# A fused attention and feed-forward kernel: a new order on all five queues, the branch turned, xn's high half on VectorE, dummy products at the start, a tail by tile

## The chip, the cores and the metric

The kernel runs on one core of one Trainium2 chip. The metric is the device time of one execution in microseconds. The core's engines are TensorE (PE, with its weight loads PEld), VectorE (DVE), ScalarE (ACT), GpSimd (POOL) and SyncE (SP), which here issues all DMAs. Each has its own queue and works it off in order; they meet through semaphores.

## What is computed

For sixteen sequences of 512 rows with 128 features, float32:

```python
x = x + layernorm(attention(layernorm(x)))       # scores = (xn*w_lhs) @ (xn*w_rhs)^T, softmax, @ xn
h = silu(t(x2, w1) * s1) * (t(x2, w2) * s2)      # x2 = layernorm(x), 128 -> 512
h = gelu(t(h, h1) * sh1)                         # 512 -> 512
h = gelu(t(h, h2) * sh2)                         # 512 -> 512
x = x + layernorm(t(h, w3) * s3)                 # 512 -> 128
```

`t` multiplies by a matrix whose entries are -1, 0 or 1. There is no gain or bias in the layer norms.

## The kernel before

Every sequence b is one unit of work of N = 16; it is held as T = 4 tiles of 128 rows, and the hidden 512 features as K = 4 blocks of 128. To keep float32 accuracy each operand of a product is split into a high half that the array takes exactly and a low remainder: ScalarE makes the high half by a copy (`high_xT`, `high_aT`, `high_e`, `high_A`, `high_x2T`, the first of the two instructions of each `gelu`), VectorE or GpSimd the low one by a subtraction (`low_xT`, `low_aT`, `low_e`, `low_A`, `low_B`, `low_x2T` on VectorE, `low_C` and `low_xn` on GpSimd), and TensorE adds the products (`product`, L341).

The path of one sequence: SP loads x (`load_x`); VectorE takes statistics (`x_statistics`, `aggregate`), GpSimd the reciprocal root (`rstd`, L1995), VectorE normalises by tile (`normalize_x`, L1579), TensorE turns the tiles (`turn_x`), and `scores` (L309) makes four 128x512 blocks of scores, three products each. VectorE takes each block's row maximum (`row_max`), ScalarE the exponential (`softmax`), TensorE turns the result (`turn_e`), and `attend` (L325) multiplies it with xn, split into two fp16 halves: `xn_hi` (GpSimd's `high_xn`, L2014) and `xn_lo`. Both exist once, so `high_xn(b)` waits (`wait_free` on `pv_done`) until all `attend` of sequence b - 1 are done. Then come a layer norm (`attention_statistics`, `rstd_att`, `normalize_att`), the sum x1 (`add_attention`), another norm (`normalize_x1`), `turn_x2`, and the feed-forward part: `gated` (L356, four products into a pair of banks; `silu` on ScalarE, `gated` on VectorE), `layer1` and `layer2` (sixteen pairs of products each, `gelu1`, `gelu2` between), `layer3`, `scale_y`, `turn_y`, the last norm and `add_ffn` on GpSimd, and `store`. ScalarE loads a table at each change between exponential, silu and gelu.

The work of neighbouring sequences is interleaved in an order written out by hand for every engine: `start()`, then a loop `Fori(5, N - 3)` over `step(i)`, whose calls belong to the sequences i to i - 4 (`now`, `back1`, ...; `ahead` on VectorE), then `finish()`. Nothing reorders a queue at run time. On TensorE `start()` stands before a branch: the sum of the weights' low bits (`sum_lo` on ScalarE for each of six parts of the weights, `gather_lo`, `total_lo`) is loaded into a register; it is zero for these weights; if it weren't, `main(general=True)` would run, with a third product per pair. `main` holds `ramp()`, the loop and `finish()`, and both bodies are in the program one behind the other:

```python
pe.wait_ge(lo_known, 1)
any_lo = pe.value_load(lo_total[0:1, 0:1].bitcast(i32))
with pe.If(any_lo != 0):
    main(general=True)
with pe.Else():
    main(general=False)
```

SP's `start()` issues x(0), x(1), x_res(0), the columns and then the six parts of the weights (512 KB each but the last, which has 256 KB; an x has 256 KB, the columns 9.5 KB). ScalarE's `start()` begins with `sum_lo(0)`, `high_xT(0)`, `high_aT(0)`. At the end the last sequence goes through `layer3` with `low_C` on GpSimd, `turn_y`, `y_statistics`, `rstd`, `normalize_y`, `add_ffn` of the whole [128, 4, 128] tile, and one store.

## Time and profile before

| what | value |
|---|---|
| median of 3 runs | 511.75 us (511.27 to 512.38) |
| the profiled execution | 512.09 us |
| its span, first to last instruction | 510.3 us |
| PE busy | 479.0 us, 94%, 2818 products |
| ACT busy | 447.9 us, 88% |
| DVE busy | 384.9 us, 75% |
| POOL busy | 245.7 us, 48% |
| mean granted clock of TensorE | 0.986 |

The span and what lies around it (1.8 us) make the execution's time. Busy products overlap each other on TensorE, so its pace is read from their starts. Times in the rows count from the span's start.

### The profile page before, as it was taken

How to read it: one execution, taken by the hardware profiler on the slowest of the kernel's cores; microseconds unless marked ns; L12 is line 12 of the kernel's file. 1: busy time of each engine (PE TensorE's matmuls, PEld its weight loads, DVE VectorE, ACT ScalarE, POOL GpSimd, SP SyncE). 2: the span in 40 equal slices, each digit the busy share in tenths (PEclk: the TensorE clock that was granted, in tenths of full speed). 3: DMA queues.
4: the chain of work that ended last, by engine and by line, in shares of the span. 5: the costliest groups of instructions: out<-in, count | busy, mean ns of one | idle time of the engine just before them, and what ended most of it. 6: DMA issues, size and time to landing. Idle time of an engine off the chain costs nothing.

```text
span 510.3 us, 9417 instructions
## 1 busy us (share of the span) xinstructions
PE 479.0 (94%) x2818; PEld 385.3 (76%) x2818; DVE 384.9 (75%) x1154; ACT 447.9 (88%) x749; POOL 245.7 (48%) x270
## 2 busy tenths in 40 slices
PE   2959999999999999999999999999999999999992
PEld 1747888888888888888888888878787788787771
DVE  4968979697786969698686969878688777475552
ACT  4968999998999999898999999898989999786771
POOL 3635773634445473535455453445624316143444
PEclk9979999999999999999999999999999999999997
DMA  8020101202011100202121110111101100010111
GB/s 299 12 85 1 63 1 42 83 2 102 21 62 41 62 21 22 81 21 62 41 62 38 42 44 21 63 41 43 62 4 59 42 3 21 1 62 2 62 43 62
DMA packets 12557, 24.23 MB, mean 47 GB/s; under 512 B 1520, under 2 KB 1520, under 8 KB 12528
## 3 DMA queue, kind: packets, MB, share of 16 engines
q1 hardware_dynamic: 12528, 23.87, 14.0%
q8 instruction: 15, 0.25, 0.2%
q14 instruction: 14, 0.11, 0.1%
HBM read 15.48 MB, written 8.39 MB: 47 GB/s over the span
## 4 chain that ended last, share of the span: by engine, by line
PE 81%; ACT 9%; issue 4%; DVE 3%; DMA 1%; POOL 1%; SPq 0%; POOLq 0%; ACTq 0%; DVEq 0%
PE hid_bank L345 21%; PE hid_bank L347 21%; PE score_bank L294 5%; PE mix_bank L331 3%; PE hid_bank L366 3%; PE mix_bank L332 3%; PE mix_bank L335 3%; PE score_bank L313 3%; PE hid_bank L371 2%; PE hid_bank L370 2%; PE hid_bank L367 2%; PE score_bank L319 2%; PE score_bank L316 2%; PE w_bank L303 2%; PE w_bank L347 2%
## 5 line engine op out<-in xcount | busy, mean ns | idle before, releaser
L345 PE MATMUL hid_bank<-hA_hi,w_hi 128*128 128x512 f32 x256 | 105.9, 414 | 1.2 <-DVE hA_full L1503 1.2
L345 PE MATMUL hid_bank<-hB_hi,w_hi 128*128 128x512 f32 x256 | 105.3, 412 | 1.6 <-DVE hB_lo L1577 1.6
L347 PE MATMUL hid_bank<-hB_lo,w_hi 128*128 128x512 f32 x256 | 101.1, 395 | 0.0
L347 PE MATMUL hid_bank<-hA_lo,w_hi 128*128 128x512 f32 x256 | 100.7, 393 | 0.0
L2026 POOL TENSOR_TENSOR hC_lo<-hC_full,hC_hi 128x512 fp32r<-128x512 f32 x64 | 81.2, 1294 | 22.9 <-ACT hC_full L1163 22.8
L1499 DVE TENSOR_REDUCE neg_max<-score_bank 128x1 f32<-128x512 f32 x56 | 38.3, 687 | 41.6 <-PE score_bank L319 40.6
L1503 DVE SCALAR_TENSOR_TENSOR hA_full<-hid_bank,columns,gate 128x512 f32<-128x512 f32 x64 | 46.7, 746 | 19.1 <-ACT gate L1156 18.3
L345 PEld LDWEIGHTS hid_bank<-hB_hi,w_hi 128*128 128x128 f32 x256 | 48.2, 188 | 11.7 <-DVE hB_lo L1577 2.7
L345 PEld LDWEIGHTS hid_bank<-hA_hi,w_hi 128*128 128x128 f32 x256 | 48.2, 188 | 11.5 <-DVE hA_full L1503 2.5
L347 PEld LDWEIGHTS hid_bank<-hB_lo,w_hi 128*128 128x128 f32 x256 | 48.4, 189 | 9.7 <-DVE hB_lo L1577 0.9
L1998 POOL TENSOR_SCALAR ln_y_var_eps<-ln_y_mean_var 128x4 f32<-128x4 f32 x16 | 5.8, 360 | 102.1 <-DVE ln_y_mean_var L1494 102.1
L347 PEld LDWEIGHTS hid_bank<-hA_lo,w_hi 128*128 128x128 f32 x256 | 48.3, 189 | 8.6
L1577 DVE TENSOR_TENSOR hB_lo<-hid_bank,hB_hi 128x512 fp32r<-128x512 f32 x64 | 43.4, 680 | 13.4 <-ACT hid_bank L1163 13.1
L1162 ACT ACT_TABLE_LOAD x29 | 37.2, 1283 | 16.1 <-PE hid_bank L347 15.7
L1162 ACT ACTIVATE hC_hi<-hid_bank,columns 128x512 fp32r<-128x512 f32 x64 | 44.6, 697 | 7.4 <-PE hid_bank L347 6.0
L1162 ACT ACTIVATE hB_hi<-hid_bank,columns 128x512 fp32r<-128x512 f32 x64 | 44.8, 701 | 3.7 <-PE hid_bank L347 3.4
L1573 DVE TENSOR_TENSOR hA_lo<-hA_full,hA_hi 128x512 fp32r<-128x512 f32 x64 | 44.1, 693 | 1.1 <-ACT hA_hi L1143 0.9
L1163 ACT ACTIVATE hC_full<-hid_bank,columns 128x512 f32<-128x512 f32 x64 | 44.4, 693 | 0.0
L1156 ACT ACTIVATE gate<-hid_bank,columns 128x512 f32<-128x512 f32 x64 | 42.4, 685 | 2.2 <-PE hid_bank L371 1.8
L1163 ACT ACTIVATE hid_bank<-hid_bank,columns 128x512 f32<-128x512 f32 x64 | 43.1, 673 | 0.0
L1131 ACT ACT_TABLE_LOAD x28 | 35.9, 1283 | 6.4 <-DVE neg_max L1499 5.3
L1569 DVE TENSOR_TENSOR eT_lo<-score_bank,eT_hi 128x512 f16<-128x512 f32 x56 | 38.2, 682 | 3.5 <-ACT eT_hi L1137 3.5
(105 smaller groups left out, 1216.8 us busy)
## 6 DMA issues: line engine op xcount, KB each, us to landing
x_res<-x_dram SPq DMA_DIRECT2D x16, 256.0 KB, 2.8
out_dram<-x SPq DMA_DIRECT2D x16, 256.0 KB, 2.0
x_tail<-out_dram SPq DMA_DIRECT2D x16, 256.0 KB, 3.0
out_dram<-y_out SPq DMA_DIRECT2D x16, 256.0 KB, 2.0
x_in<-x_dram SPq DMA_DIRECT2D x15, 256.0 KB, 2.6
w_raw<-weights_dram SPq DMA_DIRECT2D x5, 512.0 KB, 5.9
x_ahead<-x_dram SPq DMA_DIRECT2D x1, 256.0 KB, 2.9
w_raw<-weights_dram SPq DMA_DIRECT2D x1, 256.0 KB, 5.7
```

The source lines that it names most:

```text
L345: nc.tensor.matmul(bank[:, :], w_hi[:, w], hi, start=first, stop=False)
L347: mm = nc.tensor.matmul(bank[:, :], w_hi[:, w], lo, start=False, stop=last and not general)
L1131: nc.scalar.activation(exps[:, j, :], score_home(b, j)[:, :], ACT.Exp, bias=neg_max[:, j:j + 1], scale=-1.0, accum_out=row_sum[:, j:j + 1] ...
L1156: nc.scalar.activation(gate[:, m % 2, :], hid_bank[2 * (m % 2)][:, :], ACT.Silu, scale=columns[:, S1 + m:S1 + m + 1]).then_inc(gate_ready, 1)
L1162: nc.scalar.activation(hi[:, m, :], hid_bank[m][:, :], ACT.Gelu, scale=scale)
L1163: nc.scalar.activation(full, hid_bank[m][:, :], ACT.Gelu, scale=scale).then_inc(done, 1)
L1499: nc.vector.tensor_reduce(neg_max[:, j:j + 1], score_home(b, j)[:, :], AX.X, ALU.min).then_inc(max_ready, 1)
L1503: nc.vector.scalar_tensor_tensor(hA_full[:, m, :], hid_bank[2 * (m % 2) + 1][:, :], columns[:, S2 + m:S2 + m + 1], gate[:, m % 2, :], ALU. ...
L1569: nc.vector.tensor_tensor(eT_lo[:, j, :, :].rearrange("p t s -> p (t s)"), score_home(b, j)[:, :], eT_hi[:, j, :, :].rearrange("p t s -> p ...
L1573: nc.vector.tensor_tensor(hA_lo[:, m, :], hA_full[:, m, :], hA_hi[:, m, :].bitcast(f32), ALU.subtract).then_inc(hA_lo_ready, 1)
L1577: nc.vector.tensor_tensor(hB_lo[:, m, :], hid_bank[m][:, :], hB_hi[:, m, :].bitcast(f32), ALU.subtract).then_inc(hB_lo_ready, 1)
L2026: nc.gpsimd.tensor_tensor(hC_lo[:, m, :], hC_full[:, m, :], hC_hi[:, m, :].bitcast(f32), ALU.subtract).then_inc(hC_lo_ready, 1)
```

## The change

All queues get a new order. Beside the order these parts are new: the branch is turned; `warm_up` puts dummy products before and behind the first turn; `high_xn` moves from GpSimd to VectorE; the last sequence's `low_C` moves to VectorE, and its last norm, sum and store go tile by tile. Six pieces move ahead of the branch: `scores(2, 0)`, `scores(2, 1)`, `attend(1, 2)`, `attend(1, 3)`, `turn_e(2, 0)` and `turn_x2(0)`. The loop of every engine is cut at another place: an iteration of TensorE's begins with `layer1(back4, 0, 0)` and ends with `turn_y(back4)`.

```diff
@@ SP
+            def store_tiles(g):
+                for t in range(T):
+                    sp.wait_ge(y_tile_ready, t + 1)
+                    sp.dma_start(x_view(out_dram, g)[:, t, :], y_out[:, t, :]).then_inc(out_stored, 16)
             def start():
                 load_x(0)
-                load_x(1)
-                load_x_res(0)
                 load_columns()
                 load_weights(0)
+                load_x(1)
                 load_weights(1)
                 load_weights(2)
+                load_x(2)
                 load_weights(3)
-                load_x(2)
+                load_x_res(0)
                 load_weights(4)
                 load_weights(5)
...
-                store(N - 1)
+                store_tiles(N - 1)
@@ TensorE
+            def warm_up(count):
+                for _ in range(count):
+                    nc.tensor.matmul(score_bank[0][:, 0:P], ident[:, :], ident[:, :], start=True, stop=True)
             def start():
+                warm_up(11)
                 turn_x(0)
+                warm_up(5)
                 scores(0, 0)
...
                 attend(1, 0)
+                turn_e(1, 2)
+                scores(2, 0)
+                turn_e(1, 3)
+                attend(1, 1)
                 gather_lo()
-                attend(1, 1)
-                turn_e(1, 3)
+                scores(2, 1)
+                attend(1, 2)
+                attend(1, 3)
+                turn_e(2, 0)
+                pe.wait_ge(xT_lo_ready, 6)
+                turn_x2(0)
@@ TensorE, step(i): the head and the end of the new loop
+                    pe.wait_ge(gated_done, back4 * K + 3)
+                    layer1(general, back4, 0, 0)
+                    pe.wait_ge(gated_done, back4 * K + 3)
+                    layer1(general, back4, 1, 0)
                     layer1(general, back4, 0, 1)
+                    pe.wait_ge(yT_ready, back1 - 3)
+                    turn_x(back1)
...
                     gated(general, back3, 3)
+                    pe.wait_ge(e_lo_ready, back1 * T + 2)
+                    scores(back1, 3)
                     pe.wait_ge(att_n_ready, back4 + 3)
                     turn_y(back4)
@@ TensorE, the branch
-            with pe.If(any_lo != 0):
+            with pe.If(any_lo == 0):
+                main(general=False)
+            with pe.Else():
                 main(general=True)
-            with pe.Else():
-                main(general=False)
@@ VectorE
+            def high_xn(b):
+                dve.wait_ge(xn_ready, b + 1)
+                wait_free(dve, pv_done, T, b, 0)
+                nc.vector.tensor_copy(xn_hi[:, :, :], xn[:, :, :]).then_inc(xn_hi_ready, 1)
+            def low_C(b, m):
+                dve.wait_ge(hC_lo_ready, b * K)
+                dve.wait_ge(gelu2_done, b * K + m + 1)
+                nc.vector.tensor_tensor(hC_lo[:, m, :], hC_full[:, m, :], hC_hi[:, m, :].bitcast(f32), ALU.subtract).then_inc(hC_lo_ready, 1)
+            def normalize_and_add_y(b):
+                dve.wait_ge(ln_y.rstd_ready, b + 1)
+                dve.wait_ge(y_ready, b)
+                dve.wait_ge(x1_tail_loaded, b * 16 + 16)
+                dve.wait_ge(out_stored, b * 16)
+                for t in range(T + 1):
+                    if t < T:
+                        nc.vector.tensor_scalar(y_n[:, t, :], y_bank[:, t * P:(t + 1) * P], ln_y.mean_var[:, t, 0:1],
+                                                ln_y.rstd[:, t:t + 1], ALU.subtract, ALU.mult).then_inc(y_tile_normalized, 1)
+                    if t > 0:
+                        dve.wait_ge(y_tile_normalized, t)
+                        nc.vector.tensor_tensor(y_out[:, t - 1, :], y_n[:, t - 1, :], x1_tail[:, t - 1, :],
+                                                ALU.add).then_inc(y_tile_ready, 1)
@@ VectorE, step(i): what follows aggregate(ln_x, ahead) in the new loop
+                low_e(back1, 2)
+                low_xT(now)
+                low_e(back1, 3)
                 low_aT(now)
                 low_B(back3, 1)
+                low_B(back3, 2)
+                high_xn(now)
+                row_max(now, 0)
+                low_B(back3, 3)
+                row_max(now, 1)
+                attention_statistics(back1)
                 normalize_x1(back2, 0)
                 normalize_x1(back2, 1)
+                normalize_x(ahead, 0)
@@ VectorE, finish()
+                low_C(N - 1, 0)
+                low_C(N - 1, 1)
+                low_C(N - 1, 2)
+                low_C(N - 1, 3)
                 y_statistics(N - 1)
                 aggregate(ln_y, N - 1)
-                normalize_y(N - 1)
+                normalize_and_add_y(N - 1)
@@ GpSimd
-            def high_xn(b):
-                pool.wait_ge(xn_ready, b + 1)
-                wait_free(pool, pv_done, T, b, 0)
-                apart(pool)
-                nc.gpsimd.tensor_copy(xn_hi[:, :, :], xn[:, :, :]).then_inc(xn_hi_ready, 1)
@@ ScalarE, start(): the head
                 sum_lo(0)
                 high_xT(0)
                 high_aT(0)
                 sum_lo(2)
-                high_weights(2)
-                sum_lo(1)
+                high_weights(0)
                 softmax(0, 0)
-                high_weights(5)
                 softmax(0, 1)
                 softmax(0, 2)
```

In the finish two places of the order matter to the prediction. Between `gated(N - 6, 0)` and `gated(N - 6, 2)` stand now `scores(N - 4, 2)` and `scores(N - 4, 3)` (before: neither), between `gated(N - 5, 0)` and `gated(N - 5, 2)` stands `scores(N - 3, 2)` (before: `turn_e(N - 3, 1)`), and between `gated(N - 4, 0)` and `gated(N - 4, 2)` no scores and no `turn_e` (before: `scores(N - 2, 2)` and `turn_e(N - 2, 1)`). ScalarE's `softmax(N - 1, 0)` and `softmax(N - 1, 1)` stand between `silu(N - 3, 1)` and `silu(N - 3, 2)` (before: between two gelus).

## Rows read from the trace of the kernel before

**Rows 1.** Windows: stretch, length, busy us per engine (instructions), PEclk, DMA share, GB/s.
```profile
0.00:15.00 15.00, 6.06 (x15) 4.04 (x16) 7.79 (x30) 8.38 (x15) 5.21 (x15) 1.00 0.74 263
30.00:40.00 10.00, 4.85 (x36) 4.10 (x35) 5.97 (x20) 5.57 (x9) 3.56 (x4) 0.66 0.34 105
80.00:320.00 240.00, 240.00 (x1454) 196.50 (x1453) 194.19 (x595) 226.81 (x379) 118.69 (x131) 1.00 0.14 45
320.00:460.00 140.00, 137.40 (x810) 109.99 (x807) 105.61 (x297) 126.23 (x210) 60.46 (x67) 1.00 0.11 37
460.00:502.00 42.00, 38.57 (x167) 29.04 (x165) 19.92 (x57) 30.43 (x48) 19.82 (x19) 1.00 0.09 32
```

**Rows 2.** Timeline of TensorE, the turn of y in two iterations six apart.
```profile
135.09 0.60 PE L294 MATMUL mix_bank<-ident,yT 128*128 128x128 f32 x4
310.18 0.60 PE L294 MATMUL mix_bank<-ident,yT 128*128 128x128 f32 x4
```

**Rows 3.** Timeline of the first 13 us: start, us, engine, line, tiles.
```profile
1.21 0.29 POOL L2050 TENSOR_SCALAR_AFFINE_SELECT ident<-ident 128x128 f32<-128x128 f32 x1
4.96 0.87 DVE L1484 BATCH_NORM_STATS2 ln_x_stats<-x_ahead 128x6 f32<-128x128 f32 x4
6.40 1.12 DVE L1584 TENSOR_SCALAR xn<-x_in,ln_x_mean_var,ln_x_rstd 128x128 f32<-128x128 f32 x4 [0.57 <-POOL ln_x_rstd L2011]
6.89 1.15 PE L303 MATMUL w_bank<-ident,xn 128*128 128x128 f32 x4 [6.89 <-DVE xn L1584]
7.83 1.06 ACT L1190 ACTIVATE hA_full<-w_raw 128x1024 f32<-128x1024 uint16 x1 [5.61 <-DMA w_raw<-weights_dram]
10.08 0.69 DVE L1479 TENSOR_TENSOR xT_lo<-w_bank,xT_hi 128x512 fp32r<-128x512 f32 x1 [1.76 <-ACT aT_hi L1124]
12.07 0.63 PE L313 MATMUL hid_bank<-xT_hi,aT_hi 128*128 128x512 f32 x1
12.50 0.63 PE L316 MATMUL hid_bank<-xT_lo,aT_hi 128*128 128x512 f32 x1
```

**Rows 4.** Timeline of VectorE and TensorE around the branch, 32 to 41 us.
```profile
32.21 1.11 DVE L1592 TENSOR_SCALAR x2n<-x,ln_x_mean_var,ln_x_rstd 128x128 f32<-128x128 f32 x4
35.40 0.79 PE L313 MATMUL score_bank<-xT_hi,aT_hi 128*128 128x512 f32 x1 [5.15 <-issue]
37.09 0.69 DVE L1499 TENSOR_REDUCE neg_max<-score_bank 128x1 f32<-128x512 f32 x1 [3.77 <-PE score_bank L319]
38.56 0.69 DVE L1479 TENSOR_TENSOR x2T_lo<-w_bank,x2T_hi 128x512 fp32r<-128x512 f32 x1 [0.18 <-ACT x2T_hi L1183]
39.97 0.39 PE L367 MATMUL hid_bank<-x2T_hi,w_hi 128*128 128x512 f32 x1
40.20 0.40 PE L370 MATMUL hid_bank<-x2T_lo,w_hi 128*128 128x512 f32 x1
```

**Rows 5.** Groups by form, whole run: busy us, mean ns, idle before.
```profile
L1592 DVE TENSOR_SCALAR x2n<-x,ln_x_mean_var,ln_x_rstd 128x128 f32<-128x128 f32 x64 | 19.0, 341 | 0.1
L2026 POOL TENSOR_TENSOR hC_lo<-hC_full,hC_hi 128x512 fp32r<-128x512 f32 x64 | 81.2, 1294 | 22.9 <-ACT hC_full L1163 22.8
L2018 POOL CAST xn_hi<-xn 128x512 f16<-128x512 f32 x16 | 9.8, 613 | 35.2 <-PE mix_bank L335 18.7 <-issue 15.2 <-DVE xn L1584 1.3
L1162 ACT ACT_TABLE_LOAD x29 | 37.2, 1283 | 16.1 <-PE hid_bank L347 15.7
```

**Rows 6.** TensorE's waits from 320 to 502 us: total, times, longest.
```profile
PE hid_bank L366 <- DVE hA_full L1503: 2.3, 3, 1.0
```

**Rows 7.** Timeline of the last 12 us, four engines.
```profile
498.13 0.68 ACT L1163 ACTIVATE hC_full<-hid_bank,columns 128x512 f32<-128x512 f32 x1
500.20 0.49 PE L347 MATMUL w_bank<-hC_lo,w_hi 128*128 128x512 f32 x1 [0.84 <-POOL hC_lo L2026]
505.17 1.36 DVE L1523 TENSOR_SCALAR y_n<-mix_bank,ln_y_mean_var,ln_y_rstd 128x128 f32<-128x128 f32 x4 [1.52 <-POOL ln_y_rstd L2011]
507.90 0.34 SPq L213 DMA_DIRECT2D out_dram<-y_out  x1
```

More of the change, by code:

```diff
@@ L525, in ramp @@
                     gated(general, 1, 0)
+                    pe.wait_ge(gelu2_done, 4)
+                    gated(general, 1, 1)
                     pe.wait_ge(x2T_lo_ready, 2)
@@ L1715, in start @@
-                low_A(1, 2)
-                low_A(1, 3)
-                aggregate(ln_y, 0)
-                x_statistics(5)
-                low_xT(4)
-                normalize_y(0)
-                normalize_x1(2, 1)
-                low_e(3, 2)
-                low_B(1, 0)
-                aggregate(ln_x, 5)
-                low_aT(4)
-                low_B(1, 1)
-                low_e(3, 3)
-                normalize_x1(2, 2)
-                row_max(4, 0)
-                scaled_eps(3)
-                normalize_x1(2, 3)
@@ L1732, in start @@
-                row_max(4, 1)
+                low_A(1, 2)
+                aggregate(ln_y, 0)
+                low_A(1, 3)
+                x1_statistics(2)
+                x_statistics(5)
+                normalize_y(0)
+                aggregate(ln_x1, 2)
+                low_B(1, 0)
+                low_e(3, 2)
+                low_xT(4)
+                low_e(3, 3)
+                low_aT(4)
+                scaled_eps(3)
+                low_B(1, 1)
+                aggregate(ln_x, 5)
+                high_xn(4)
@@ L1847, in finish @@
                 gated(N - 5, 3)
-                row_max(N - 3, 2)
                 low_A(N - 5, 2)
                 row_max(N - 3, 3)
-                normalize_x1(N - 4, 1)
-                y_statistics(N - 6)
-                low_A(N - 5, 3)
-                aggregate(ln_y, N - 6)
-                x_statistics(N - 1)
-                low_xT(N - 2)
-                scaled_eps(N - 3)
-                aggregate(ln_x, N - 1)
-                normalize_y(N - 6)
-                low_B(N - 5, 0)
-                low_e(N - 3, 2)
@@ L1862, in finish @@
-                low_aT(N - 2)
-                low_B(N - 5, 1)
-                low_e(N - 3, 3)
+                y_statistics(N - 6)
+                aggregate(ln_y, N - 6)
+                low_A(N - 5, 3)
+                x1_statistics(N - 4)
+                low_xT(N - 2)
+                aggregate(ln_x1, N - 4)
+                low_e(N - 3, 2)
+                normalize_y(N - 6)
+                x_statistics(N - 1)
+                scaled_eps(N - 3)
+                normalize_x1(N - 4, 0)
+                normalize_x1(N - 4, 1)
@@ L1865, in finish @@
+                low_B(N - 5, 0)
+                low_aT(N - 2)
+                normalize_x1(N - 4, 2)
+                normalize_x1(N - 4, 3)
+                low_e(N - 3, 3)
+                low_B(N - 5, 1)
+                aggregate(ln_x, N - 1)
+                row_max(N - 2, 0)
+                row_max(N - 2, 1)
                 low_B(N - 5, 2)
-                row_max(N - 2, 0)
                 low_B(N - 5, 3)
-                row_max(N - 2, 1)
                 attention_statistics(N - 3)
-                normalize_x1(N - 4, 2)
@@ L1883, in finish @@
+                high_xn(N - 2)
+                low_A(N - 4, 0)
+                gated(N - 4, 2)
+                gated(N - 4, 3)
+                low_A(N - 4, 1)
+                row_max(N - 2, 2)
+                normalize_x(N - 1, 0)
+                low_A(N - 4, 2)
+                low_A(N - 4, 3)
+                y_statistics(N - 5)
+                x1_statistics(N - 3)
+                low_B(N - 4, 0)
                 low_e(N - 2, 1)
+                normalize_x(N - 1, 1)
+                low_B(N - 4, 1)
@@ L2091, in step @@
                 back2 = i - 2
+                back3 = i - 3
                 back4 = i - 4
-                rstd(ln_x, now)
-                high_xn(back1)
-                low_xn(back1)
-                rstd_att(back2)
-                low_C(back4, 0)
-                low_C(back4, 1)
-                low_C(back4, 2)
                 low_C(back4, 3)
```

1121 lines of the change are left out of this document (540 added, 581 removed).

## The prediction, made before the changed kernel was run

> **What bounds the kernel now.** I read the windows of the whole run first [rows 1]. From 80 to 320 us TensorE is busy 240.0 of 240.0 us, while ScalarE has 226.8 us of work in them, VectorE 194.2 and GpSimd 118.7. So the middle is TensorE's throughput, and only its own work or a wait of its own can change it. One sequence takes there (310.18 - 135.09) / 6 = 29.18 us [rows 2], and sixteen of them are 467 us. The span is 510.3 us, so some 43 us lie elsewhere, and the windows say where: TensorE is idle 9 of the first 15 us, 5 of the ten from 30 to 40 us, some 3 of 320 to 460, over 3 of 460 to 502, and nearly all of the last 8 to 9 us. The change can earn something in the ramp, in the finish and in the tail, and lose something in all four parts.
>
> The ramp in order of time. The first product of a score waits for the first block of weights: ScalarE's queue begins with a sum over w_raw, which starts when that lands, at 7.83, and holds back ScalarE's two copies of the turned x; VectorE's xT_lo waits for the second, aT_hi, until 10.08 [rows 3]. Products there start 0.43 us apart (12.07 to 12.50), 0.23 later on (39.97 to 40.20), the slower of the clock's two levels against the faster [rows 3, 4]. From then on VectorE is hardly idle until its last x2n tile ends at 32.21 + 1.11 = 33.3. At 30.2 TensorE reaches the branch on the weights' low bits, and its next product starts at 35.40 after 5.15 us in which it waited for nothing that the profile shows; VectorE then idles 3.77 us for that product's result, and the granted clock over 30 to 40 us is 0.66 [rows 1, 4]. The first feed-forward group's second product starts at 39.97.
>
> **The change part by part.** My sum is against the profiled execution, 512.09 us (span 510.3 and 1.8 around it), 0.34 above the median of the three runs, 511.75.
>
> Branch. With the condition turned, the general=False body follows the branch directly and the branch moves behind turn_x2(0). What remains of the 5.15 us there is unknown: at most all of it, at least the register load alone. I take the lower end, under 1 us, and it is covered: after turn_x2(0) TensorE must wait for ScalarE's copy and VectorE's difference (some 0.6 and 0.7 us) anyway. The Trainium skill, "Runtime: NRT & Kernel Launch", section "Instruction fetch mechanics", says that a taken branch out of the fetched pages stalls for a fetch and that sequential code is fetched ahead; by that rule only the old order pays. At the end of the program TensorE now must jump over the other body; it has 8.4 us for that while the tail runs (501.9, some 1.7 us behind the product on hC_lo, to 510.3), against 5.15 us, so this costs nothing, and with no tail it would cost the 5.
>
> But the 5.15 us are not all gained, for VectorE is late next. VectorE's low_x2T(0) ends before at 38.56 + 0.69 = 39.25, and the third product of gated(0,0), which needs it, starts at 40.20 [rows 4]. In the new order VectorE finishes the first four tiles at 7.5, then does the negated weights (0.3, an estimate like one tile's instruction), statistics (0.9), high_xn(0) (0.5) and an aggregate (0.4, a third of four such tiles' 1.11): low_xT(0) at 9.6 instead of 10.1 [rows 3, 4], if the first weights land before the turn is done. They should: 256 KB + 9.5 KB stand before them instead of three times 256 KB and 9.5 KB. From low_xT(0) to its last x2n tile the old order needs 33.3 - 10.1 = 23.2 us [rows 3, 4]. The new one needs these and, before low_x2T(0): high_xn(1) and (2) at 0.5 each, row_max(2,0), row_max(2,1) and low_e(1,3) at 0.6, one more set of statistics 0.9, and low_x2T 0.7, which is 27.6. It ends at 37.2, and the third product can start there instead of at 40.20: 3.0 us. By then TensorE has also done scores(2,1) and turn_e(2,0), three products at 0.23 and four turns at some 0.1, which before stood behind: 1.1 us more work done. Ramp: 3.0 + 1.1 = 4.1 us. The ends are 1.5 (GpSimd's or ScalarE's queue is late in it) and 6 (VectorE's new order has fewer holes than the old one's 23.2 us).
>
> Dummy products. Eleven before the first turn and five behind it, on the identity, into a score bank that nobody uses yet. They lie between 1.5 us (identity ready) and 6.89, when the first tile is there, and then in the hole of over 2 us before aT_hi. Nearest rows: a turn at the slower level, 1.15/4 = 0.29, and a full product there, 0.43 [rows 3]; at 0.43 eleven take 4.7 us and are done at 6.3. So they cost nothing; if each takes 0.86 (two full passes), eleven end at 11 and push the first turn by 4 us. Their gain is the faster level from about 7 us, 0.2 us on each of the 9 products until 15, nearly all of it hidden behind VectorE's row maxima.
>
> The moved rounding. GpSimd's cast of 0.61 us becomes a VectorE copy. Bounds: one normalised 128x128 tile, 0.34, and a 512-wide difference, 0.69 [rows 3, 5]. I take 0.5. Sixteen are 8 us on an engine that is idle 46 us of the 240. The Trainium skill, "VectorE: DVE Perf Modes", section "The perf-mode tier table (the rule you actually need)", lets an fp32 copy in SBUF run at twice the rate of a two-input operation; by it the copy would be near the lower end and the ramp 0.3 us shorter. GpSimd loses 0.61 us of 29.18 that nobody waited for. The new wait matters more: high_xn(now) waits in VectorE's queue for all attend of the sequence before, and behind it stand low_B(back3,3) and the row maxima. Writing the new loop beside TensorE's order at 0.23 a product, attend ends about 12 us into the iteration, VectorE comes to the copy at about 12.5, and low_B(.,3) is wanted at 16. Nothing is lost, with 2 us of cover. The tighter hand-overs of the loop, low_A(.,3) before layer1(.,0,3), low_aT before scores and low_e(.,3) before attend(.,3), have 0.5 us each. Counted in the code, the loop keeps nine groups of short products among the long ones, as before, and five table loads. So I leave 29.18 us.
>
> Finish. The largest of TensorE's waits there are three, 2.3 us in all, at gated(.,2) for VectorE's gate [rows 6]. In the first two sequences of the new finish a scores group (0.7 us) stands between gated(.,0) and gated(.,2) that stood before them, or behind; in the third the filler is 1.1 us thinner. ScalarE gets one more table load of 1.28 us (73 in the old order, 74 in the new, counted in the code) [rows 5]. I take a gain of 0.5, with ends -2 and +2.5.
>
> Tail. low_C(N-1,.) moves from GpSimd (1.29) to VectorE (0.69): the last hC_full ends at 498.81, the product on hC_lo starts at 500.20 [rows 5, 7], and would at 498.9 + 0.7 = 499.6: 0.6. Normalising begins at 505.17 and takes 1.36 us, and behind it the whole-tile sum on GpSimd some 1.3, for the store is issued at 507.90; interleaved on VectorE, four tiles at 0.34 and four sums at 0.2 (my estimate: a third of the 0.69 for a quarter of its columns) end at 507.35: 0.5. The store takes from 507.90 to the end; a last piece of 64 KB instead of 256 KB gives between 0 and 0.5, I take 0.3. Sum 1.4. SP issues each piece in 0.34 us [rows 7] while VectorE needs 0.5 a tile, so its queue isn't late.
>
> Sum: 4.1 + 0.5 + 1.4 = 6.0; 512.1 - 6.0 = 506.1.
>
> **The rivals.** (1) VectorE binds in the loop. For: in its order the long stretch from gated(.,2) to the row maxima has no hole for 16 us and hand-overs of 0.5. Against: it is idle 19% from 80 to 320 us. If 0.3 us a sequence leaks in eight loops and three of the finish, 3.3 us go: 509.4. (2) Slower: at high_xn's wait. Its place is VectorE's queue between low_B(.,2) and low_B(.,3). It decides if attend ends over 2 us later against VectorE than I count, or if the stretch behind it runs 0.5 us late and ScalarE, with 94.5% of the time in work, can't make it good. At 0.7 us a sequence in eleven it costs 7.7: 513.8. (3) The branch costs as before, because it is the register load or the branch itself and not where it leads. Then 5 us stand before gated(0,0) with 1.3 of cover, and the slower clock again 1.5; the ramp loses 1 instead of gaining 4: 511. The Trainium skill's "SBUF — State Buffer", on the shared port pair, lets a two-port VectorE copy block GpSimd for its length; by it each early copy could hold a reciprocal root by up to 0.5 us, and the ramp would gain 3.1. (4) Better: ramp 6, finish 2, tail 1.6: 502.5.
>
> **How the numbers follow.** Forecast 506.1 with 0.55; (1) 0.15; (2) 0.08; (3) 0.06; (4) 0.16. The range leaves out (2), half of (3) and the best end of (4): 502.4 to 510.5. Under 0.2%, 1.0 us, a measurement here can't tell from no change. Faster is all of the forecast, (1) and (4), less a little: 0.85; same mostly (3): 0.07; slower 0.08.
>
> **What would show it.** Right: a gap of under 1.5 us around the branch and products 0.23 apart behind it; gated(0,0) near 37; turn_y to turn_y still 29.18; xn_hi on VectorE near 0.5; the last store issued near 502. Wrong: TensorE waits between 80 and 320 us (rival 1 or 2, told apart by whether VectorE idles before xn_hi); 5 us at the branch (3); the first turn later than 6.9 (dummies too long).

## The result, and the profile of the kernel after

| what | before | after |
|---|---|---|
| median | 511.61 us (511.27 to 512.38, 4 runs) | 508.32 us (508.14 to 508.9, 4 runs) |
| the profiled execution | 512.09 us | 508.16 us |
| its span | 510.3 us | 506.4 us |
| mean granted clock | 0.986 | 0.991 |
| first product of gated(0,0) | 39.64 us | 34.88 us |
| period of the loop | 29.18 us | 29.47 us |

The change is faster by 0.7%: ratio 0.993, 95% interval 0.9916 to 0.9944. The forecast was 506.1 (502.4 to 510.5); the profiled execution stands 2.1 us above it. 3.9 us of span were gained and not 6.0.

The windows that answer to [rows 1], and that from 15 to 30 us, kernel after (stretch, length, busy us per engine, PEclk, DMA share, GB/s):

```profile
0.00:15.00 15.00, 12.32 (x68) 10.06 (x68) 9.23 (x33) 9.22 (x18) 4.44 (x13) 1.00 0.74 263
15.00:30.00 15.00, 12.39 (x97) 9.83 (x96) 14.51 (x46) 13.68 (x29) 8.42 (x8) 0.89 0.12 29
30.00:40.00 10.00, 9.18 (x83) 7.45 (x82) 9.75 (x40) 9.31 (x18) 5.96 (x6) 1.00 0.18 66
80.00:320.00 240.00, 240.00 (x1463) 194.16 (x1462) 194.65 (x594) 222.10 (x374) 114.17 (x124) 1.00 0.14 44
```

From 30 to 40 us TensorE is busy 9.2 us instead of 4.9. From 80 to 320 us it is "busy" all 240.0 in both kernels, and yet an iteration got longer: busy products overlap, so a wait of 0.1 to 0.2 us between two of them doesn't show in this column. Only the starts show it. The turn of y in two iterations seven apart, timeline of TensorE, kernel after:

```profile
100.99 0.60 PE L299 MATMUL mix_bank<-ident,yT 128*128 128x128 f32 x4
...
307.29 0.60 PE L299 MATMUL mix_bank<-ident,yT 128*128 128x128 f32 x4
```

(307.29 - 100.99) / 7 = 29.47 us, against 29.18 in [rows 2]: 0.29 us lost in each of eight iterations.

The ramp, timeline of the kernel after, the first 13 us (compare [rows 3]):

```profile
1.57 4.54 PE L410 MATMUL score_bank<-ident 128*128 128x128 f32 x22 [1.57 <-POOL ident L2091]
...
6.03 1.06 ACT L1201 ACTIVATE hA_full<-w_raw 128x1024 f32<-128x1024 uint16 x1 [3.80 <-DMA w_raw<-weights_dram]
...
8.15 0.41 DVE L1594 CAST xn_hi<-xn 128x512 f16<-128x512 f32 x1
...
9.01 0.69 DVE L1489 TENSOR_TENSOR xT_lo<-w_bank,xT_hi 128x512 fp32r<-128x512 f32 x1 [0.16 <-ACT aT_hi L1135]
...
10.75 0.40 PE L318 MATMUL hid_bank<-xT_hi,aT_hi 128*128 128x512 f32 x1
...
10.99 0.39 PE L321 MATMUL hid_bank<-xT_lo,aT_hi 128*128 128x512 f32 x1
```

Eleven dummies are 22 instructions and end at 6.1 us, the copy of xn takes 0.41, xT_lo starts at 9.0 instead of 10.1, and the first scores' products start 0.23 to 0.24 apart (0.43 in [rows 3]). Around the branch, timeline of VectorE and TensorE, kernel after (compare [rows 4]):

```profile
32.47 1.11 DVE L1621 TENSOR_SCALAR x2n<-x,ln_x_mean_var,ln_x_rstd 128x128 f32<-128x128 f32 x4
...
33.46 0.60 PE L308 MATMUL w_bank<-ident,x2n 128*128 128x128 f32 x4
...
34.77 0.69 DVE L1489 TENSOR_TENSOR x2T_lo<-w_bank,x2T_hi 128x512 fp32r<-128x512 f32 x1
34.88 0.47 PE L371 MATMUL hid_bank<-x2T_hi,w_hi 128*128 128x512 f32 x1 [0.82 <-ACT x2T_hi L1194]
...
35.51 0.50 PE L375 MATMUL hid_bank<-x2T_lo,w_hi 128*128 128x512 f32 x1
```

The branch lies between 33.46 and 34.88, and what TensorE waits for there is ScalarE's x2T_hi. In the trace's records of control instructions the register load takes 0.49 us (at 33.62) and the compare-and-branch 0.09 (at 34.17); before they took 0.57 and 4.67. The branch back to the loop's head, which is taken too but leads less far, takes 0.21 to 0.25 us in both kernels. At the end of the program the jump over the other body takes 3.28 us, from 498.19, while the tail runs. The third product of gated(0,0) starts at 35.51 and not at 40.20.

The tail, timeline of the kernel after (compare [rows 7]):

```profile
496.80 0.50 PE L352 MATMUL w_bank<-hC_lo,w_hi 128*128 128x512 f32 x1 [0.30 <-DVE hC_lo L1628]
...
501.79 0.73 DVE L1566 TENSOR_SCALAR y_n<-mix_bank,ln_y_mean_var,ln_y_rstd 128x128 f32<-128x128 f32 x2 [1.53 <-POOL ln_y_rstd L2058]
...
502.74 2.02 SPq L219 DMA_DIRECT2D out_dram<-y_out  x4
...
503.47 0.49 DVE L1570 TENSOR_TENSOR y_out<-y_n,x_tail 128x128 f32<-128x128 f32 x2
```

**Where the time went.** Spans against spans: turn_y(1) comes at 100.99 instead of 105.89, and by then the new order has also done the three products of a scores block (0.70 us) that stood behind it: 5.6 us ahead, with one loop iteration in it, so the ramp gained 5.9. The eight iterations lost 8 x 0.29 = 2.3. From turn_y(8) to the last product it is 191.7 us before and 191.2 after; with the 0.70 of the scores block off, that is 0.2 lost, although low_C on VectorE gave 0.5 there: the finish itself lost 0.7. Behind the last product 8.39 us became 7.85: 0.5. Sum 5.9 - 2.3 - 0.7 + 0.5 + 0.5 = 3.9.

### The profile page after: what moved, and what is told of

Same layout as the page of the kernel before. It is cut to its first block, busy times and chain, and to the rows that moved or that the text cites. A ratio compares the mean times of both kernels' runs of the same rounds, so it can differ in the third digit from the quotient of the medians.

```text
span 506.4 us, 9435 instructions
## 1 busy us (share of the span) xinstructions
PE 486.3 (96%) x2850; PEld 387.8 (77%) x2850; DVE 394.4 (78%) x1178; ACT 447.9 (88%) x750; POOL 228.8 (45%) x249
## 3 DMA queue, kind: packets, MB, share of 16 engines
HBM read 15.48 MB, written 8.39 MB: 47 GB/s over the span
## 4 chain that ended last, share of the span: by engine, by line
PE 70%; ACT 13%; DVE 11%; issue 4%; DMA 1%; POOL 0%; POOLq 0%; DVEq 0%; ACTq 0%
PE hid_bank L350 19%; PE hid_bank L352 18%; PE score_bank L299 4%; ACT hC_full L1174 3%; PE hid_bank L371 3%; PE score_bank L318 3%; PE mix_bank L340 2%; PE hid_bank L375 2%; PE mix_bank L336 2%; PE hid_bank L376 2%; PE hid_bank L372 2%; PE w_bank L308 2%; PE mix_bank L337 2%; PE w_bank L352 2%; PE score_bank L321 2%
## 5 line engine op out<-in xcount | busy, mean ns | idle before, releaser
L350 PE MATMUL hid_bank<-hB_hi,w_hi 128*128 128x512 f32 x256 | 104.0, 406 | 1.3 <-DVE hB_lo L1606 1.2
L2067 POOL TENSOR_TENSOR hC_lo<-hC_full,hC_hi 128x512 fp32r<-128x512 f32 x60 | 76.4, 1293 | 30.0 <-ACT hC_full L1174 29.9
L352 PEld LDWEIGHTS hid_bank<-hB_lo,w_hi 128*128 128x128 f32 x256 | 48.3, 189 | 10.7 <-DVE hB_lo L1606 1.2
L1173 ACT ACT_TABLE_LOAD x29 | 37.2, 1283 | 16.6 <-PE hid_bank L352 16.4
L1602 DVE TENSOR_TENSOR hA_lo<-hA_full,hA_hi 128x512 fp32r<-128x512 f32 x64 | 45.4, 715 | 0.7 <-ACT hA_hi L1154 0.5
L1174 ACT ACTIVATE hid_bank<-hid_bank,columns 128x512 f32<-128x512 f32 x64 | 44.2, 691 | 0.0
```

The costliest lines, as they stand in the source:

```text
L350: nc.tensor.matmul(bank[:, :], w_hi[:, w], hi, start=first, stop=False)
L352: mm = nc.tensor.matmul(bank[:, :], w_hi[:, w], lo, start=False, stop=last and not general)
L1173: nc.scalar.activation(hi[:, m, :], hid_bank[m][:, :], ACT.Gelu, scale=scale)
L1174: nc.scalar.activation(full, hid_bank[m][:, :], ACT.Gelu, scale=scale).then_inc(done, 1)
L1602: nc.vector.tensor_tensor(hA_lo[:, m, :], hA_full[:, m, :], hA_hi[:, m, :].bitcast(f32), ALU.subtract).then_inc(hA_lo_ready, 1)
L2067: nc.gpsimd.tensor_tensor(hC_lo[:, m, :], hC_full[:, m, :], hC_hi[:, m, :].bitcast(f32), ALU.subtract).then_inc(hC_lo_ready, 1)
```

## The experiments

Twelve kernels ran. Each leaves out nothing of the computation. Ratios are against the kernel before on the same chip. "Period" is the loop's period, read as above from the turns of y; "g0" is the start of gated(0,0).

**e1: ScalarE's high_e(back1, 0) earlier.** In the loop of the kernel after, VectorE waits 26.9 us in 8 iterations for eT_hi.

```diff
                 gelu2(back4, 0)
-                gelu2(back4, 1)
                 high_e(back1, 0)
+                gelu2(back4, 1)
                 high_x2T(back3)
```

> The changed kernel with one line of ScalarE's loop moved: high_e(back1, 0) ahead of gelu2(back4, 1) instead of behind it. Theory A (the loop's 29.47 us instead of 29.18 come from that hand-over: VectorE stands 3.4 us before low_e(back1, 0) and scores(back1, 2) starts late): the iteration goes back to 29.2 us, eight iterations give 2.2 us, so 506.0 to 506.3. Theory B (VectorE has too much work since it has the copy to fp16, rival 1 of the prediction): the iteration stays at 29.4 to 29.5 and the time at 508.3. Theory C (nine groups of short products stand in places with dearer weight loads): also 29.4 or more.

Measured: 507.87 us (507.17 to 508.55), ratio 0.9924 (0.9907 to 0.9941); period 29.464. The first wait went, the time did not. Another took its place in every iteration, at the second pair of the feed-forward gate. Timeline of e1, VectorE and TensorE:

```profile
155.97 1.41 DVE L1513 SCALAR_TENSOR_TENSOR hA_full<-hid_bank,columns,gate 128x512 f32<-128x512 f32 x2 [1.45 <-ACT gate L1167]
...
156.32 0.40 PE L352 MATMUL w_bank<-hC_lo,w_hi 128*128 128x512 f32 x1
156.77 0.50 PE L371 MATMUL hid_bank<-x2T_hi,w_hi 128*128 128x512 f32 x1
157.11 0.40 PE L372 MATMUL hid_bank<-x2T_hi,w_hi 128*128 128x512 f32 x1
```

The two products at 156.32 and 156.77 start 0.45 apart, 0.22 more than a pair without a wait: gated(back3, 2) needs the bank that VectorE's multiplication at 155.97 reads. Also the next start is 0.34 behind it and not 0.23.

**e2: the branch not turned, all else as after.**

```diff
-            with pe.If(any_lo == 0):
-                main(general=False)
-            with pe.Else():
-                main(general=True)
+            with pe.If(any_lo != 0):
+                main(general=True)
+            with pe.Else():
+                main(general=False)
```

> The changed kernel with the branch as before it (general=True first, the other body behind Else). If the 5.15 us belong to where the branch leads, a hole of some 5 us opens behind the register load at 34.2 us, of which 0.6 us are covered by the wait for x2T_hi, and the products behind it run at the slower level of the clock for some us: 512.5 to 514.5. If the stall was the register load or the place of the branch, nothing changes: 508.3.

Measured: 511.79 us (510.35 to 513.42), ratio 0.9998 (0.9983 to 1.0014), g0 37.18, turn_y(0) at 75.41 instead of 71.46. The branch takes 3.34 us, the register load 0.48. Without the turned branch the whole change gives nothing that can be measured.

**e3: no dummy products.**

```diff
-                warm_up(11)
                 turn_x(0)
-                warm_up(5)
                 scores(0, 0)
```

> The changed kernel without the sixteen dummy products. By my prediction's step (VectorE's row maxima hide the gain) 0.3 us or less is lost: 508.3 to 508.6. If the faster level in the first 13 us carries the ramp's surplus over my forecast (6.2 us instead of 4.1), 1.5 us or more is lost: 509.8 to 510.5.

Measured: 509.94 us (508.77 to 510.62), ratio 0.9957 (0.9941 to 0.9973), g0 37.57, turn_y(0) at 74.17. Timeline of TensorE in e3:

```profile
9.18 0.80 PE L318 MATMUL hid_bank<-xT_hi,aT_hi 128*128 128x512 f32 x1 [1.26 <-ACT aT_hi L1133]
...
12.01 0.63 PE L324 MATMUL hid_bank<-xT_hi,aT_lo 128*128 128x512 f32 x1
12.44 0.63 PE L318 MATMUL hid_bank<-xT_hi,aT_hi 128*128 128x512 f32 x1
...
14.57 0.63 PE L324 MATMUL hid_bank<-xT_hi,aT_lo 128*128 128x512 f32 x1
```

The start is the same (9.18 against 9.03), but the last of the first twelve score products starts at 14.57 instead of 12.6: at 3 x 0.43 = 1.3 us a block, where a row maximum takes 0.6. So in this ramp TensorE, not VectorE, is the slow one between 9 and 15 us. The ratio says 1.4 us and g0 2.7; the same ramp gave g0 between 34.3 and 35.8 in the profiles of e1, e8, e9 and e11, so this one is good for a size of 1.4 to 2.7.

**e4: xn_hi back on GpSimd.**

```diff
-            def high_xn(b):
-                dve.wait_ge(xn_ready, b + 1)
...
+            def high_xn(b):
+                pool.wait_ge(xn_ready, b + 1)
+                wait_free(pool, pv_done, T, b, 0)
+                apart(pool)
+                nc.gpsimd.tensor_copy(xn_hi[:, :, :], xn[:, :, :]).then_inc(xn_hi_ready, 1)
```

> The changed kernel with high_xn taken back to GpSimd, each directly ahead of its low_xn there. If VectorE's added work is what the loop lost (theory B), the iteration falls to 29.2 us: 506.3. If the hand-over of high_e is the cause (theory A), the iteration stays at 29.47 and the time at 508.3 or a little less, as VectorE's copy of 0.41 us is hidden; GpSimd's 0.61 us ahead of rstd_att and low_C can also cost up to 1 us in ramp or finish: 507.8 to 509.3.

Measured: 507.38 us (507.01 to 508.53), ratio 0.992 (0.9903 to 0.9938), period 29.467, g0 34.48. The copy on VectorE is not what lengthens the loop, and moving it earned nothing that can be measured. The g0 lies within the scatter of this ramp. By the Trainium skill, "SBUF — State Buffer", section "Who interferes with whom", a two-port copy of VectorE and a GpSimd instruction contend for a shared pair of ports: the one that is issued first has it for its whole length, and the other waits. No run here shows the copy holding up GpSimd. The other way round it is there once in the kernel after, timeline of GpSimd and VectorE:

```profile
51.04 4.72 POOL L2085 TENSOR_TENSOR w_lo<-w_raw,w_hi 128x1024 fp32r<-128x1024 f32 x2
...
55.15 0.89 DVE L1594 CAST xn_hi<-xn 128x512 f16<-128x512 f32 x1
```

This copy starts while GpSimd works and takes 0.89 us instead of 0.41 to 0.43; it ends 0.28 us behind GpSimd's operation (55.76), and so it does, by 0.28 to 0.29, in e1, e2, e3, e8, e9 and e11. That agrees with the rule.

**e5, e6, e7: one part each, put on the kernel before.** Branch turned alone; tail by tile with low_C on VectorE alone; dummies alone. e5 is e2's diff the other way round, e7 e3's. e6:

```diff
-                store(N - 1)
+                store_tiles(N - 1)
...
-                normalize_y(N - 1)
+                normalize_and_add_y(N - 1)
```

> The kernel before with the branch turned and nothing else. VectorE and ScalarE idle 3.8 and 4.2 us behind the branch there, but low_aT(2) ends only at 32.3, so scores(2, 0) can start at 31.1 and its third product at 32.3 instead of 36.4, and the clock stays at the faster level: a gain of 3 to 4.5 us, 507.2 to 508.7. If so, the branch alone gives about what the whole change gave. If the stall is the register load, 511.6.

> The kernel before with low_C(N-1, .) on VectorE and the last norm, sum and store by tile. My step was 1.4 us: 510.2. From the trace after, where the span from the last turn to the end is 7.9 instead of 8.4 us and the wait for hC_lo 0.3 instead of 0.8: 1.0 to 1.1, so 510.5.

> The kernel before with the sixteen dummy products. Its turned x waits for ScalarE's sum over the first weights anyway, and VectorE's maxima follow one another: 0 to 0.8 us gained, 510.8 to 511.6.

Measured: e5 508.64 us (508.17 to 509.29), ratio 0.9944 (0.9922 to 0.9966), g0 34.95, period 29.197. e6 510.73 (509.18 to 512.3), ratio 0.9981 (0.9966 to 0.9996), span 508.9, which is 1.4 us less (0.2 of it by turn_y(1), where e6 is the kernel before; 0.6 before and 0.7 behind the last product belong to the tail). e7 511.92 (511.02 to 512.92), ratio 0.9999 (0.9984 to 1.0014), g0 39.10. The branch alone brings gated(0,0) 4.7 us forward, of which 3.9 are left at the end of the span (0.5 of the rest go behind the last product, which no run takes apart); window of e5, 30 to 40 us, against 4.85 and 0.66 in [rows 1]:

```profile
30.00:40.00 10.00, 8.62 (x59) 6.54 (x58) 9.47 (x29) 9.70 (x16) 7.32 (x6) 1.00 0.31 105
```

In the old ramp the dummies are worth nothing that can be measured.

**e8, e9: the chain through the row maximum shortened.** In the loop of the kernel after ScalarE waits 10.7 us in 7 iterations for neg_max. e8 moves one block of scores, e9 has e1's edit too.

```diff
                     attend(back2, 2)
-                    attend(back2, 3)
                     pe.wait_ge(e_lo_ready, back1 * T - 1)
                     scores(back1, 0)
+                    attend(back2, 3)
```

> The kernel after, with scores(back1, 0) put one attend earlier in TensorE's loop (ahead of attend(back2, 3), where the old loop has it). Theory A, a ring: row_max(back1, 0) and with it softmax(back1, 0) come some 0.7 us earlier in every iteration, ScalarE's wait for neg_max (10.7 us in 7 iterations, 1.5 each) falls to about 0.8, high_e(back1, 0) ends 0.7 earlier, TensorE's late starts at scores(back1, 2) and gated(back3, 2) go, and the period from turn_y to turn_y falls from 29.47 to 29.2: 2 us less over the loop. Theory B, the new loop's period is set by the order of its products (exposed weight loads between short and long ones), not by a chain: the period stays within 0.05 of 29.47, whatever ScalarE waits.

> Both edits on the kernel after: scores(back1, 0) ahead of attend(back2, 3), and high_e(back1, 0) ahead of gelu2(back4, 1). By itself the second left the period at 29.46, since a wait of 0.2 us at gated(back3, 2) took the place of the one at scores(back1, 2). Theory A (ring): with the scores early too neither wait is left, and the period is 29.2 or less, the time some 505.9 against 508.3 of the kernel after. Theory B (order of products): 29.4 or more.

Measured: e8 509.23 us (508.76 to 510.14), ratio 0.9955 (0.994 to 0.9969), period 29.557; e9 509.65 (508.04 to 510.09), ratio 0.9955 (0.9941 to 0.9969), period 29.567. The loop got 0.09 us longer. Two things show. First, one more block of long products after short ones costs 0.09 us: the second of its products starts 0.31 us behind the first, not 0.23. Second, the scores came 0.7 us earlier, but the row maximum didn't. VectorE in e9, timeline:

```profile
143.16 0.43 DVE L1594 CAST xn_hi<-xn 128x512 f16<-128x512 f32 x1 [0.86 <-PE mix_bank L340]
143.50 0.68 DVE L1509 TENSOR_REDUCE neg_max<-score_bank 128x1 f32<-128x512 f32 x1
```

Here the moved rounding does hold VectorE up, for the end of attend(back2, 3), and the row maximum queues behind it. This is the prediction's rival at high_xn's wait, made real by 0.7 us of other order; in the kernel after VectorE waits only 0.1 us there (0.08 to 0.12).

**e11, e12: that hold-up taken away.** e11 is e9 with the row maximum ahead of the copy; e12 is e9 with the copy on GpSimd.

```diff
                 low_B(back3, 2)
-                high_xn(now)
                 row_max(now, 0)
+                high_xn(now)
                 low_B(back3, 3)
```

> As e9 (scores(back1, 0) ahead of attend(back2, 3), high_e(back1, 0) ahead of gelu2(back4, 1)), and on VectorE row_max(now, 0) ahead of high_xn(now). In e9 VectorE idles 0.86 us before xn_hi, for the end of all attend, and row_max(.,0) stands behind it, at 143.50 against 143.37 in the kernel after: the early scores earned nothing. Theory A (ring through scores, row maximum, softmax, with the moved copy as the hold-up in e9): row_max(.,0) starts some 1 us earlier, ScalarE's wait for neg_max falls from 13.1 us to under 7 in 7 iterations, the wait at gated(back3, 2) goes, and the period is 29.30 (floor of before 29.19 plus 0.09 for one more entry from short into long products). Theory B (only the order of the products counts): 29.56 as in e8 and e9. If the copy's late end now delays something instead (turn of the pair attend, low_xn), the period is above 29.56.

> As e9, with high_xn on GpSimd as in the kernel before, so that nothing waits for the end of all attend in VectorE's queue. Theory A: as e11, period 29.30, and the ramp of the run with the rounding on GpSimd (first gated product at 34.5, first turn_y at 70.4): some 506 us. Theory B: period 29.56, 508.5 us.

Measured: e11 509.06 us (508.42 to 510.37), ratio 0.9942 (0.9927 to 0.9956), period 29.568; e12 507.65 (507.42 to 508.62), ratio 0.9922 (0.9907 to 0.9937), period 29.581. The row maximum now starts 1.0 us earlier in the iteration than in e9, and the softmax too (14.39 us behind turn_y instead of 15.39); ScalarE's wait for neg_max fell from 13.1 to 6.1 us. The period did not move. So theory A, that the chain scores, row maximum, softmax sets the loop, falls. Theory B gave the right number for e8, e9, e11 and e12, one more entry into long products; whether it also explains the 0.29 us is for the next section. ScalarE, VectorE and TensorE in e11, timeline:

```profile
148.78 1.28 ACT L1173 ACT_TABLE_LOAD   x1 [1.15 <-PE hid_bank L352]
...
157.91 1.41 DVE L1513 SCALAR_TENSOR_TENSOR hA_full<-hid_bank,columns,gate 128x512 f32<-128x512 f32 x2 [1.45 <-ACT gate L1167]
...
158.71 0.50 PE L371 MATMUL hid_bank<-x2T_hi,w_hi 128*128 128x512 f32 x1
```

What came earlier is spent in a wait of 1.15 us ahead of the table load of gelu2, for TensorE's layer2(back4, 0, 3).

**e10: the order of before with the other three parts** (e5, e6 and e7 in one).

> The kernel before, its whole order kept, with the three parts that are not the order: branch turned, tail by tile with low_C on VectorE, sixteen dummy products. If they add up from their single runs (ratios 0.9944, 0.9981, 0.9999 of the kernel before) this gives 0.992, about 507.9, as much as the whole change, so that the new order of the queues earns nothing in all. If the new order earns something (by the kernel after's ramp, y0 at 71.5 against 74.2) this stands above 508.5. Period 29.2 by all theories.

Measured: 507.05 us (505.61 to 507.19), ratio 0.991 (0.9888 to 0.9931), period 29.195. Timeline of TensorE in e10, turns of y seven iterations apart:

```profile
100.45 0.60 PE L300 MATMUL mix_bank<-ident,yT 128*128 128x128 f32 x4
...
304.82 0.60 PE L300 MATMUL mix_bank<-ident,yT 128*128 128x128 f32 x4
```

Its interval overlaps that of the change (0.9916 to 0.9944), so the whole times leave it open whether e10 is the faster of the two. By the medians 1.3 us lie between them. Between the profiled executions it is more, 503.7 against 506.4 us of span, but e10's is its fastest, 1.4 us below its median, and the kernel after's ran 3.4 us of the ramp at a granted clock of 0.50, e10's none. Against before, e10 has 5.4 us by turn_y(1), loses 0.1 in the loop, and has 0.5 before and 0.7 behind the last product: 6.6 in all. The kernel after has 5.9, loses 2.3 in the loop and 0.2 up to the last product, and has 0.5 behind it. So the new order is worth some 0.5 us in the ramp and costs some 2.2 us in the loop and 0.7 in the finish; the two have no other difference but where xn is rounded, which by e4 is worth nothing that can be measured.

## Why the loop is 0.29 us longer

Theory B, the order of products, doesn't give it. Both loops have nine entries from short into long products, and the second product starts there 0.31 to 0.32 us behind the first in both, instead of 0.23. Start to start, in the mean of seven iterations, the new loop loses 0.14 us at the first product of scores(back1, 2) and 0.10 at its second, and 0.05 at all other places together. The first two are a wait, which e1 removes, and another takes its place. So something else holds TensorE. With theory A fallen, the traces leave this reading. Timeline of the kernel after, ScalarE, VectorE and TensorE, in one iteration, from layer2(back4, 0, 3), whose second product is at 146.85, to gated(back3, 2) at 157.27:

```profile
146.85 0.40 PE L352 MATMUL hid_bank<-hB_lo,w_hi 128*128 128x512 f32 x1
...
147.33 1.28 ACT L1173 ACT_TABLE_LOAD   x1 [0.38 <-PE hid_bank L352]
...
150.92 0.60 ACT L1148 CAST eT_hi<-score_bank 128x512 f16<-128x512 f32 x1
...
151.39 0.63 ACT L1194 CAST x2T_hi<-w_bank 128x512 fp32r<-128x512 f32 x1
...
151.91 0.40 PE L352 MATMUL hid_bank<-hB_lo,w_hi 128*128 128x512 f32 x1
152.30 0.50 PE L318 MATMUL score_bank<-xT_hi,aT_hi 128*128 128x512 f32 x1
...
154.35 1.28 ACT L1164 ACT_TABLE_LOAD   x1
...
156.47 1.41 DVE L1513 SCALAR_TENSOR_TENSOR hA_full<-hid_bank,columns,gate 128x512 f32<-128x512 f32 x2 [1.20 <-ACT gate L1167]
...
157.27 0.50 PE L371 MATMUL hid_bank<-x2T_hi,w_hi 128*128 128x512 f32 x1
```

The same place in the kernel before, its layer2(back4, 0, 3) at 182.92 and 183.15:

```profile
181.05 0.58 ACT L1183 CAST x2T_hi<-w_bank 128x512 fp32r<-128x512 f32 x1
181.51 0.60 ACT L1137 CAST eT_hi<-score_bank 128x512 f16<-128x512 f32 x1
182.13 1.28 ACT L1162 ACT_TABLE_LOAD   x1
...
183.15 0.39 PE L347 MATMUL hid_bank<-hB_lo,w_hi 128*128 128x512 f32 x1
...
183.58 0.69 ACT L1162 ACTIVATE hC_hi<-hid_bank,columns 128x512 fp32r<-128x512 f32 x1 [0.16 <-PE hid_bank L347]
...
191.50 0.49 PE L366 MATMUL hid_bank<-x2T_hi,w_hi 128*128 128x512 f32 x1
```

In the old loop ScalarE makes both copies and loads gelu's table while TensorE is still at this product, and only the activation waits for it, 0.16 us. In the new one TensorE comes to the product earlier, but the two copies stand behind it, and so does the table load: ScalarE waits ahead of the load (0.38 us) and not between load and activation. In the trace's records the wait is an instruction of its own there, at 147.28, and the activation carries another wait; in the old loop the activation itself carries the wait for TensorE, and the other one rides on a register instruction before.

From the load on ScalarE has no hole until the gate. From that load to gated(back3, 2) it is 9.93 to 9.95 us in the kernel after and in e1, e8, e9, e11 and e12, whatever was moved upstream of it and wherever TensorE's wait stood; that constancy is the evidence. From 146.85 to 157.27 are 10.42 us, of which 10.15 are left for TensorE's own work once its waits are taken off. It waits in the kernel after at scores(back1, 2), for low_e(back1, 0) (at 152.30, 0.39 behind its neighbour, 0.16 more than without a wait), so that at gated(back3, 2) it is just in time; where e1's edit removes that wait, it waits 0.22 us at gated(back3, 2). The product behind scores' late one comes 0.34 and not 0.23 later. 0.16 + 0.11 is 0.27 in this iteration (0.24 in the mean); the rest of the 0.29 lies in spacings of hundredths. In e1, e9, e11 and e12 the wait at gated(back3, 2) is for VectorE's multiplication, and that waits for ScalarE's gate (1.45 us in e1 and e11), so the chain ends in the wait that is left. What makes the chain long, the place of the two copies and of the load, is argued from these rows and not shown by a run that shortens it.

Not tried, and so not shown: gelu's table loaded ahead of the wait by a dummy activation, as `silu` does with `table_loader`, or the two copies back ahead of gelu2(back4, 0). The first could start the load up to 0.38 us earlier in the kernel after, more than the wait is long.

## Why the prediction was right, and where it was wrong

**Faster, within the range, 2.1 us too low.** Four of its terms were off: the ramp gave 1.8 us more than forecast, and the loop took 2.3, the finish 1.2 and the tail 0.4 that were not in the sum. That it is off by no more than 2.1 is in part luck, and the median, 508.3, is nearer to rival (1)'s 509.4 than to the forecast. The last store is issued at 504.33 and not near 502, by the same 2 us.

**Branch: right.** The cost that was to be "under 1 us, and it is covered" is 0.49 + 0.09 us between turn_x2(0) and a product that waits for ScalarE anyway. e2 prices it in the new kernel at 3.5 us, e5 in the old at 2.9 (1.7 to 4.0), by the ratios. What costs is where the branch leads: the taken branch took 3.3 to 4.7 us in the four kernels that have it ahead of gated(0,0) (before, e2, e6, e7), the one not taken 0.09. The Trainium skill, "Runtime: NRT & Kernel Launch", section "Instruction fetch mechanics", has the rule that a taken branch out of the fetched pages must wait for a fetch, and here the traces agree. The DMA view of the kernel before over the branch, 30.67 to 35.34 us (queue, kind: packets, MB, share of 16 engines):

```profile
q8 instruction: 1, 0.02, 2.3%
```

This is a transfer of 16 KB of instructions, from 32.22 to 33.92. Each of the four taken branches has such a transfer inside it (e2 34.67 to 35.63, e6 32.03 to 32.95, e7 31.88 to 32.80), and the branch not taken has none. Rival (3) falls.

At the end the jump costs TensorE nothing, as forecast, but it isn't always free. It brings two such transfers. In the kernel after the second ends at 503.43, and SP's second store issue, begun at 503.26, takes 0.54 us, against 0.33 in e2 and e6, which don't jump there. In e4 and e11 it takes 0.94 and 1.08 us, and the tail behind the last product is 8.23 and 8.37 us long, against 7.67 in e2 and e6. In e1, e10 and e12 the transfer ends by the time that the issue begins, and nothing is lost. In all four kernels with a lengthened issue of over 0.5 us (after, e4, e9, e11) it ends 0.37 to 0.39 us behind the end of the transfer. That the transfer holds it up is read from this and was not tried.

**Ramp: the largest term, mis-sized; 5.9 instead of 4.1.** The step that failed is the count from low_xT(0) to the third product, 9.6 to 37.2. low_xT(0) began at 9.0, and to the third product it took 26.5 us, not 27.6, so the third product came 4.7 us earlier and not 3.0. The sum had also priced the dummies' gain as "nearly all of it hidden behind VectorE's row maxima"; e3 shows 1.4 to 2.7 us. At 1.3 us a block against 0.6 a row maximum, TensorE sets the pace; [rows 3] had the 0.43 from which to see it. That they cost nothing was right, the last of the first eleven ends at 6.1 (forecast 6.3).

**xn's rounding: right in size, without gain.** 0.41 to 0.43 us in fifteen of sixteen copies, between the bounds 0.34 and 0.69 and below the 0.5 taken. The Trainium skill, "VectorE: DVE Perf Modes", section "The perf-mode tier table (the rule you actually need)", gives such a copy twice the rate of a two-input operation. The trace agrees in the main: 0.41 against 0.69, 1.7 times. e4 undoes the move and is not slower. The wait that rival (2) feared is 0.1 us long in the kernel after; e9 shows it at 0.86 when attend ends 0.7 us later. So the rival had its place right, and the cover, which the prediction put at 2 us, is nearly nil for the copy itself; no one was late by it because the row maximum behind it had to wait 0.3 us more for its scores.

**Loop: the step that failed.** "So I leave 29.18 us" came from counting groups of short products and table loads. Both counts were right (as many entries, as many loads), and the leak was elsewhere: TensorE waits, by the reading above, for what stands behind one wait on ScalarE. The prediction's own sign of it, waits of TensorE between 80 and 320 us, doesn't show in the busy time, which is 240.0 of 240.0; it takes the starts. I had checked the hand-overs of VectorE and not the stretch from layer2(., 0, 3) over two table loads to the gate. Rival (1) had the leak of 0.3 us to the digit, by luck, for it has the wrong engine: VectorE is idle before the late multiplication by 1.20 us, and e4, which takes the copy off it, changes nothing.

**Finish: wrong sign.** Forecast +0.5, measured -0.7. Waits of TensorE from 310 to 496 us, kernel after (total, times, longest; before, [rows 6] has the first row's counterpart):

```profile
PE hid_bank L371 <- DVE hA_full L1513: 1.3, 3, 0.6
PE hid_bank L350 <- DVE hB_lo L1606: 1.0, 2, 0.6
PE hid_bank L371 <- ACT hC_full L1174: 0.9, 2, 0.6
PE score_bank L299 <- ACT exps L1142: 0.8, 1, 0.8
```

The wait at gated(., 2) did shrink, from 2.3 to 1.3 us, as the better filler in two sequences said. But the 0.8 is new and the 0.9 was 0.2 before, and they took it back. The 0.8 is at 423.69, a turn waiting for a softmax behind the extra table load, which the prediction counted (73 and 74 in all, 74 and 75 in the traces) and did not place. All waits of this view come to 4.2 us, against 4.3 in the same stretch before, so it does not show where the 0.7 went. The starts show most of it: intervals that are 0.12 us or more longer than usual for their kind of product add up to 7.2 us after and 6.6 before, in more and shorter waits.

**Tail: 1.0 instead of 1.4** in the kernel after, 1.3 in e6, where it stands alone. low_C gives 0.5 (0.6 forecast). VectorE's part was right, 2.17 us from 501.79 to 503.96. The step that failed is "SP issues each piece in 0.34 us" and "so its queue isn't late": the four issues take 0.34 to 0.54 us and stand as a train of 2.02 us from 502.74 on. The last sum ends at 503.96, and the last issue is at 504.33, 0.37 late. Its landing takes 1.7 us, against 2.0 for the whole tile. So norm, sum and issue gave 0.2 and not 0.5, and the smaller last piece 0.4 (0.3 forecast).

## What to carry to other kernels

A busy share of 100% on the bounding engine hides waits of 0.1 to 0.2 us: compare starts of the same instruction some iterations apart. When an order is changed, follow not only who hands over to whom but what must run between two waits on one engine, table loads included: in the old loop gelu's load ran while ScalarE had to wait anyway, in the new one ScalarE first idles 0.38 us and then loads for 1.28. And take a change of many parts apart before keeping all of it: three small parts on the old order did at least as well here as the whole.

## What the runs showed that was not expected

- A compare-and-branch on TensorE that jumps far takes 3.3 to 4.7 us, with a transfer of 16 KB of instructions in it; back to the loop's head it takes 0.21 to 0.25, not taken 0.09.
- In the first 15 us PEclk reads 1.00 in before and e3 while their products start 0.43 us apart, against 0.23 with dummies. The column does not show this; the starts do.
- In the kernel after and e8 the granted clock is 0.50 for 3.4 us from 25.9 (25.8) us on, in e11 from 27.8; in e1, e4, e9 and e12 it stays at 1.00 there. g0 is 34.8 to 35.8 in the first three and 34.3 to 34.5 in the others. From 24 to 27 us TensorE is busy 1.6 us in the kernel after and 1.3 in e9, which kept its clock, but also 1.3 in e11, which did not; what decides it these rows don't show.
- The loop's wait of TensorE among long products cost its length and 0.11 us more on the next product; each block of long products behind short ones costs 0.09.
- A copy on VectorE that starts while GpSimd works on SBUF takes 0.89 us instead of 0.43.
